# The first convolution's opening tiles moved into the end of the preceding group, and the loaded images put into another buffer

## The chip, the cores and the metric

The kernel runs on one core of a Trainium2 chip. The metric is the device time of one execution in microseconds (us). A core has five engines that run their own instruction streams side by side and wait for each other through semaphores: TensorE (PE in the rows; its weight loads are PEld), VectorE (DVE), ScalarE (ACT), GpSimd (POOL) and SyncE (SP, which here issues DMAs only). Data stands in an on-chip memory of 128 partitions (tensors `sb_...`) and in an accumulation memory that TensorE writes (`ps...`).

## The reference

The input is `x`, 16 images of 32 channels of 56 x 56 pixels. Cut to what matters here:

```
xn = group_norm(x)                       # 32 groups: each channel by itself
t2 = conv(xn, w2)                        # 1x3, 32 -> 32 channels
t3 = einsum(shifted xn, xn) / 56         # 7 Gram matrices of 32 x 32 per image
t7 = depthwise 1x5 of t2;  t8 = depthwise 5x5, dilation 2, of xn
t10 = einsum(p9w * p6w * t3, t2 shifted in rows) / sqrt(32 * 7)
x = x + t8 - (t10 - t7)
t = tokens of x                          # 3136 tokens of 32 per image
t = t + attention(layer_norm(t))         # one head
t = t + mixture_of_experts(layer_norm(t))
```

The changed part is the convolution stage ahead of the attention. Nothing of what it computes changes.

## The kernel before

Three stages follow each other: `prepare` (convolutions, Gram matrices, tokens, queries and keys), `attend` and `finish`. `prepare` takes the 16 images in four groups of four, so that 4 images x 32 channels fill 128 partitions. `step(g, new, old, more)` is written once per engine; step g does the convolutions of group g and beside them the tokens, keys and queries of the old group m = g - 1. A fifth step does the tokens of the last group.

For group g the order is as follows.

1. SP loads the four images into `XI` (`load`, L280). VectorE takes their mean and variance (`sample`, `statistics`) and writes the normalised images into the padded `Xp` (`normalise`, L786, semaphore `xp_ready`).
2. SP copies `Xp` into `XS` (tensor `sb_stacks`) in 16 strips for the first half of the rows and 16 for the second (`fill_stacks(g, 0)` and `fill_stacks(g, 1)`, L303, semaphores `xs_in[0]` and `xs_in[1]`). The first half may be written only when four of the old group's output tiles are done (`conv5_full`), the second only when all seven are.
3. An image has seven tiles of 448 pixels. TensorE's `conv3(g, i)` (L376) makes tile i of `t2` in the accumulation buffer `psA`, ScalarE's `to_t2` (L535) copies it into `T2`, and SP copies `T2` into a second set of strips `T2S` (`fill_stacks2`, L310, semaphores `t2s_in`).
4. `turn_stack` (L389) transposes strips on TensorE into `psT`, ScalarE's `turned` (L547) copies them to `TT`, and `correlate` (L397) multiplies them into the Gram matrices in `psG` (`gram_done`).
5. VectorE meanwhile works on `X1`, the output: `X1 = XI + tap` (L905), four more full-image taps (`taps5`), four taps of `T2` (`taps_row`, ends with `taps_done`), and between them the layer norms of the old group's tokens.
6. `conv5(g, i)` (L416) makes the seven output tiles in `psA`, and VectorE adds each to `X1` (`add`, L876, semaphore `x1_ready`).
7. `turn_output(g)` (L435) transposes all of `X1` into tokens: 25 transposes through two halves of `psT`, which ScalarE copies out (L676, L677). VectorE's next L905 overwrites `X1` and so waits until the last of these transposes is done (`t_full`).

Keys and queries of the old group are made by `turn_keys` and `queries` (L448, L460, L461), spread over the step; `queries` of the fourth image stand between `conv5` and `turn_output`. Below, the stretch from the end of `conv5(g, 6)` to the start of L905 of group g + 1 is called a changeover. There are three: from group 0 to 1, 1 to 2 and 2 to 3.

Before the change `XI` lies in the front of `T2`. So VectorE clears the padding of `T2` again in every group after L905 (L910 to L913, `t2_zero`), and the next images may be loaded only after `taps_done` and after `T2S` is filled. A program prints the functions here.

Of the kernel before, what the change touches and what calls it, by code (L numbers as in the profile page):

```python
# [15 lines left out]
N, C, H, W = 16, 32, 56, 56  # L16
P = 128
G = P // C
NG = N // G
T = H * W  # L20
TILE = 448
NT = T // TILE
# [126 lines left out]
def prepare(nc, x, wts, scr):  # L149
# [4 lines left out]
    with ExitStack() as ctx:  # L154
# [38 lines left out]

        XI = T2[:, 0:T]

# [82 lines left out]
        def _(sp):  # L278
# [48 lines left out]
            def step(g, new, old, more):  # L327
# [19 lines left out]
                if more:  # L347
                    sp.wait_ge(taps_done, g + 1)
                    for h in range(2):
                        sp.wait_ge(t2s_in[h], (g + 1) * STRIPS)  # L350
                    load(g + 1)
# [15 lines left out]
        def _(pe):  # L367
            def conv3(g, i):

                if i in (0, 3):  # L370
                    pe.wait_ge(xs_in[i // 3], (g + 1) * STRIPS)
                if i >= 2:
                    pe.wait_ge(t2_ready, g * NT + i - 1)
# [8 lines left out]
            def turn_stack(g, n, h):  # L382
                for k in HALVES[h]:
                    u = turned_set(n, h, k)
                    if u >= 2:
                        pe.wait_ge(t_free, g * TSETS + u - 1)
                    for q in range(G):
                        a = (XTOP + 2 * (G * k + q)) * XW
                        last = nc.tensor.transpose(psT[0:GR, u % 2, q * P:(q + 1) * P], XS[:, n, a:a + GR], ident[:])  # L389
                    last.then_inc(t_full, 1)  # L390
# [72 lines left out]
            def step(g, new, old, more):  # L463
# [12 lines left out]
                if not new:  # L476
# [5 lines left out]
                    return  # L482
                for i in range(3):
                    conv3(g, i)
                turn_stack(g, 0, 0)
# [34 lines left out]
                conv5(g, NT - 1, range(0, 4))  # L520
                conv5(g, NT - 1, range(4, 7), keys_of(3))
                run(queries_of(3))
                turn_output(g)

# [7 lines left out]
        def _(act):  # L532
            def to_t2(g, i):
                act.wait_ge(conv3_full, g * NT + i + 1)
                nc.scalar.activation(yrows(T2[:], YTOP + TR * i, YLEFT),  # L535
# [3 lines left out]
            def turned(g, n, h, part=slice(None)):  # L539
                place = (h * G + n) % 2  # L540
                if h * G + n >= 2:
                    act.wait_ge(gram_done, g * 2 * G + h * G + n - 1)
                for k in HALVES[h][part]:
                    u = turned_set(n, h, k)
# [37 lines left out]
            def step(g, new, old, more):  # L582
# [32 lines left out]
                if old:  # L615
# [3 lines left out]
                                  TM.rearrange("p n k c -> p n (k c)")).then_inc(tok_out, 16)  # L619
                act.wait_ge(t2_zero, g + 1)  # L620
                for i in range(3):
                    to_t2(g, i)
                if old:
# [37 lines left out]
                if old:  # L661
# [4 lines left out]
                    high_parts(m, 3, first[3])  # L666
                    keys(m, 3, first[3])
                    query_high(m, 3, range(QSETS), first[3])
                    act.wait_ge(res_out, m * G * 16 + G * 16)
                act.wait_ge(conv5_full, g * NT + NT)  # L670
# [40 lines left out]
        def _(dve):  # L711
# [18 lines left out]
            nc.vector.memset(wqk0[:], 0.0).then_inc(w_zero, 1)  # L730
            nc.vector.memset(Xp[:], 0.0)
            nc.vector.memset(X1[:, T:NC * P], 0.0)
            nc.vector.memset(lhs10[:], 0.0).then_inc(w_zero, 1)
# [132 lines left out]
            def step(g, new, old, more):  # L866
# [34 lines left out]
                if new:  # L901
                    dve.wait_ge(xp_ready, g + 1)
                    if old:
# [3 lines left out]
                    dve.wait_ge(xi_used, g + 1)  # L907

                    inside, end = YTOP * YW + YLEFT, (YTOP + H - 1) * YW + YLEFT + W
                    nc.vector.memset(T2[:, 0:inside], 0.0)  # L910
                    nc.vector.memset(T2[:, inside + W:inside + W + (H - 1) * YW].rearrange(
                        "p (r w) -> p r w", w=YW)[:, :, 0:YW - W], 0.0)
                    nc.vector.memset(T2[:, end:YLEN], 0.0).then_inc(t2_zero, 1)  # L913
                if old:
# [990 lines left out]
```

## Time and profile before

| | |
|---|---|
| time, median of 3 runs | 2673.1 us (2671.83 to 2673.99) |
| the profiled execution's own time, and its span | 2677.21 us, 2675.4 us |
| PE busy, DVE busy, ACT busy over the span | 2394.8, 2311.7, 1592.7 us |
| start of L905 in groups 0, 1, 2, 3 | 24.11, 138.78, 250.20, 360.69 us |
| start of the fifth step's work on VectorE (the last group's tokens) | 470.06 us |

The starts of L905 show a period: one group takes 111.42 us (250.20 - 138.78) and 110.49 us (360.69 - 250.20). The first group takes 114.67 us and does no old tokens.

### The profile page before, as it was taken

How to read it: one execution, taken by the hardware profiler on the slowest of the kernel's cores; microseconds unless marked ns; L12 is line 12 of the kernel's file. 1: busy time of each engine (PE TensorE's matmuls, PEld its weight loads, DVE VectorE, ACT ScalarE, POOL GpSimd, SP SyncE). 2: the span in 40 equal slices, each digit the busy share in tenths (PEclk: the TensorE clock that was granted, in tenths of full speed). 3: DMA queues.
4: the chain of work that ended last, by engine and by line, in shares of the span. 5: the costliest groups of instructions: out<-in, count | busy, mean ns of one | idle time of the engine just before them, and what ended most of it. 6: DMA issues, size and time to landing. Idle time of an engine off the chain costs nothing. (4 is left out here: it accounts for less than half of the span.)

```text
span 2675.4 us, 46972 instructions
## 1 busy us (share of the span) xinstructions
PE 2394.8 (90%) x18454; PEld 968.7 (36%) x18454; DVE 2311.7 (86%) x4151; ACT 1592.7 (60%) x2090; POOL 408.8 (15%) x456
## 2 busy tenths in 40 slices
PE   3878888269999999999999999999999998888886
PEld 1343343112222222222222222222222223878775
DVE  5486876699999999999999999999999993899997
ACT  1153443337777777777777777777777777243333
POOL 0021111300000001000000000000000000565666
PEclk9999999569999999999999999999999999676777
DMA  7697793420202212112022022020120001233230
GB/s 170 166 268 200 209 269 120 150 60 1 61 1 61 61 68 61 39 24 61 1 61 61 1 61 58 4 61 26 37 61 1 25 25 47 76 110 103 82 108 25
DMA packets 68110, 206.29 MB, mean 77 GB/s; under 512 B 20630, under 2 KB 33554, under 8 KB 61234
## 3 DMA queue, kind: packets, MB, share of 16 engines
q1 hardware_dynamic: 64034, 185.27, 25.3%
q0 software_dynamic: 3040, 15.57, 1.6%
q8 instruction: 145, 2.38, 0.4%
q10 hardware_dynamic: 816, 2.46, 0.3%
q14 instruction: 75, 0.61, 0.1%
HBM read 80.14 MB, written 61.31 MB: 53 GB/s over the span
## 5 line engine op out<-in xcount | busy, mean ns | idle before, releaser
L1395 DVE TENSOR_REDUCE at_XM<-at_psX 128x1 f32<-128x448 f32 x2688 | 1545.9, 620 | 89.2 <-PE at_psX L1220 68.4
L1301 ACT ACTIVATE at_PR<-at_psS 128x896 f32<-128x896 f32 x1344 | 1163.6, 915 | 454.1 <-PE at_psS L1196 452.1
L1238 PE MATMUL at_psV<-at_PR,at_V 128*32 128x448 f32 x5376 | 644.4, 551 | 0.1
L1196 PE MATMUL at_psS<-at_US,at_KS 128*128 128x448 f16 x2688 | 635.8, 356 | 1.2 <-ACT at_PR L1301 0.7
L1220 PE MATMUL at_psX<-at_KS,at_US 64*128 64x448 f16 x1344 | 489.7, 364 | 65.1 <-DVE at_XM L1395 43.0
L1220 PE MATMUL at_psX<-at_KS,at_UH 64*128 64x448 f16 x1344 | 489.7, 364 | 0.0
L1220 PEld LDWEIGHTS at_psX<-at_KS,at_US 64*128 64x128 f16 x1344 | 124.5, 93 | 719.8 <-DVE at_XM L1395 660.1
L1196 PEld LDWEIGHTS at_psS<-at_US,at_KS 128*128 128x128 f16 x2688 | 201.3, 98 | 271.6 <-ACT at_PR L1301 114.6
L1358 POOL CAST at_mrow<-at_mt 7x128 f16<-7x128 f32 x64 | 18.0, 281 | 1609.9 <-DVE at_mt L1414 1256.7
L1713 POOL TENSOR_TENSOR fi_WE<-fi_WE 128x256 f32<-128x256 f32 (+1 forms) x224 | 215.0, 986 | 99.7 <-DVE fi_WE L1767 99.5
L416 PE MATMUL psA<-sb_stacks,sb_lhs 128*32 128x448 f32 x1568 | 162.2, 560 | 8.8 <-DVE sb_X L876 8.8
L1238 PEld LDWEIGHTS at_psV<-at_PR,at_V 128*32 128x32 f32 x5376 | 105.7, 108 | 133.9 <-issue 125.1
L1767 DVE TENSOR_TENSOR fi_WE<-fi_psE,fi_WT 128x512 f32<-128x512 f32 (+1 forms) x208 | 128.3, 660 | 20.0 <-PE fi_psE L1599 18.1
L1568 PEld LDWEIGHTS fi_psO<-fi_wv,fi_SUMS 128*128 128x128 f32 x750 | 142.9, 293 | 3.4 <-issue 1.7
L1568 PE MATMUL fi_psO<-fi_wv,fi_SUMS 128*128 128x33 f32 x750 | 141.7, 361 | 1.3 <-DVE fi_T L1782 1.3
L1599 PE MATMUL fi_psE<-fi_wz,fi_ZS 128*128 128x256 f16 x400 | 97.2, 351 | 39.1 <-DVE fi_WE L1767 39.1
L1220 PEld LDWEIGHTS at_psX<-at_KS,at_UH 64*128 64x128 f16 x1344 | 124.5, 93 | 0.0
L705 POOL TENSOR_TENSOR sb_TK<-sb_TK,sb_XH 128x800 f32<-128x800 f32 x13 | 43.6, 3351 | 360.3 <-DVE sb_XH L818 360.3
L389 PE MATMUL psT<-sb_ident,sb_stacks 128*124 128x128 f32 x448 | 67.7, 295 | 26.9 <-ACT sb_TT L547 26.9
L416 PEld LDWEIGHTS psA<-sb_stacks,sb_lhs 128*32 128x32 f32 x1568 | 52.9, 111 | 100.8 <-issue 87.4
L1702 ACT ACTIVATE fi_ZS<-fi_psK 128x1024 f16<-128x1024 f16 x64 | 50.1, 837 | 58.5 <-PE fi_psK L1578 58.5
L376 PE MATMUL psA<-sb_stacks,sb_lhs 128*32 128x448 f32 x448 | 48.5, 564 | 37.7 <-DMA sb_stacks<-sb_Xp 32.3
(219 smaller groups left out, 1989.4 us busy)
## 6 DMA issues: line engine op xcount, KB each, us to landing
sums<-at_O SPq DMA_DIRECT2D x16, 1568.0 KB, 6.3
fi_SUMS<-sums SPq DMA_DIRECT2D x16, 1568.0 KB, 6.7
sb_stacks<-sb_T SPq DMA_DIRECT2D x64, 270.5 KB, 7.2
sb_stacks<-sb_Xp SPq DMA_DIRECT2D x64, 248.8 KB, 7.4
sb_stacks<-sb_Xp SPq DMA_DIRECT2D x64, 248.0 KB, 6.0
sb_stacks<-sb_T SPq DMA_DIRECT2D x64, 172.5 KB, 8.1
at_KS<-key_stacks SPq DMA_DIRECT2D x32, 208.0 KB, 6.9
fi_RES<-residual SPq DMA_DIRECT2D x16, 400.0 KB, 7.2
```

The costliest lines, as they stand in the source:

```text
L389: last = nc.tensor.transpose(psT[0:GR, u % 2, q * P:(q + 1) * P], XS[:, n, a:a + GR], ident[:])
L416: last = nc.tensor.matmul(o, w, v, start=(j == 0), stop=(j == 6))
L1196: last = nc.tensor.matmul(psS[:, at % 2, k, 0:TILE], KS[:, b, (2 * c + k) * P:(2 * c + k + 1) * P], US[:, b, t * TILE:(t + 1) * TILE], sta ...
L1220: last = nc.tensor.matmul(o, u[:, c * P:(c + 1) * P], k[:, t * TILE:(t + 1) * TILE], start=True, stop=True)
L1238: last = nc.tensor.matmul(psV[C * q:C * q + C, 0:TILE], V[:, b, G * k + q, :], PR[:, (n * 2 * STEPS + 2 * q4 + q // 2) % PRS, q % 2, :], s ...
L1301: nc.scalar.activation(PR[:, f % PRS], psS[:, at % 2, :, 0:TILE], ACT.Exp).then_inc(p_ready, 1)
L1395: nc.vector.tensor_reduce(o, psX[:, (at + j) % 3, 0:TILE], AX.X, ALU.max).then_inc(x_done, 1)
L1568: last = nc.tensor.matmul(psO[:, h, q * (C + 1):(q + 1) * (C + 1)], SUMS[:, b, k * P:(k + 1) * P], wv[:], start=True, stop=True)
L1599: last = nc.tensor.matmul(psE[:, u % 2, j * EC:(j + 1) * EC], ZS[:, b, a:a + P], wz16[:, 0:EC], start=True, stop=True)
L1702: nc.scalar.activation(ZS[:, b, a:a + w], psK[:, s % 2, 0:w], ACT.Copy).then_inc(zs_ready, 1)
L1713: return nc.gpsimd.tensor_tensor(WE[:, s, 0:h, 0:w], WE[:, s, 0:h, 0:w], WE[:, s, h:2 * h, 0:w], ALU.add)
L1767: nc.vector.tensor_tensor(WE[:, u // 2, :, q:q + j].rearrange("p e k c -> p k e c"), psE[:, u % 2, 0:j * EC].rearrange("p (k e c) -> p k e ...
```

## The change

`XI` moves from `T2` into the front of `TT`, the buffer of the turned strips. `T2` is cleared once at the start and no more after that. The load of the next images waits for `gram_done` (all strips of the group read) in place of `taps_done` and `T2S`. ScalarE's first two sets of `turned` wait until L905 has read `XI` (`xi_used`), and `to_t2` of tile 0 waits for `taps_done` and `T2S` of the group before. `conv3(g + 1, 0)`, `(g + 1, 1)` and `(g + 1, 2)` with their copies are issued at the end of step g, ahead of `turn_output(g)`, and no longer at the start of step g + 1.

```diff
-        XI = T2[:, 0:T]
+        XI = TT[:].rearrange("p a q s -> p (a q s)")[:, 0:T]
...
                 if more:
-                    sp.wait_ge(taps_done, g + 1)
-                    for h in range(2):
-                        sp.wait_ge(t2s_in[h], (g + 1) * STRIPS)
+                    sp.wait_ge(gram_done, (g + 1) * 2 * G)
                     load(g + 1)
...
                 if i in (0, 3):
                     pe.wait_ge(xs_in[i // 3], (g + 1) * STRIPS)
+                if i < 2 and g > 0:
+                    pe.wait_ge(x1_ready, g * NT - 1 + i)
...
                     if u >= 2:
                         pe.wait_ge(t_free, g * TSETS + u - 1)
+                    elif g > 0:
+                        pe.wait_ge(t_free, g * TSETS)
...
-                for i in range(3):
-                    conv3(g, i)
+                if not old:
+                    for i in range(3):
+                        conv3(g, i)
                 turn_stack(g, 0, 0)
...
                 conv5(g, NT - 1, range(4, 7), keys_of(3))
+                if more:
+                    conv3(g + 1, 0)
                 run(queries_of(3))
+                if more:
+                    conv3(g + 1, 1)
+                    conv3(g + 1, 2)
                 turn_output(g)
...
             def to_t2(g, i):
+                if i == 0:
+                    act.wait_ge(t2_zero, 1)
+                    if g > 0:
+                        act.wait_ge(taps_done, g)
+                        for h in range(2):
+                            act.wait_ge(t2s_in[h], g * STRIPS)
...
                 if h * G + n >= 2:
                     act.wait_ge(gram_done, g * 2 * G + h * G + n - 1)
+                else:
+                    act.wait_ge(xi_used, g + 1)
...
-                act.wait_ge(t2_zero, g + 1)
-                for i in range(3):
-                    to_t2(g, i)
+                if not old:
+                    for i in range(3):
+                        to_t2(g, i)
...
                     keys(m, 3, first[3])
+                if more:
+                    to_t2(g + 1, 0)
+                if old:
                     query_high(m, 3, range(QSETS), first[3])
+                if more:
+                    to_t2(g + 1, 1)
+                    to_t2(g + 1, 2)
...
             nc.vector.memset(Xp[:], 0.0)
+            nc.vector.memset(T2[:], 0.0).then_inc(t2_zero, 1)
...
-                    nc.vector.memset(T2[:, 0:inside], 0.0)
-                    nc.vector.memset(T2[:, inside + W:inside + W + (H - 1) * YW].rearrange(
-                        "p (r w) -> p r w", w=YW)[:, :, 0:YW - W], 0.0)
-                    nc.vector.memset(T2[:, end:YLEN], 0.0).then_inc(t2_zero, 1)
```

TensorE at the second changeover, before: the last output tile (L416), the fourth image's queries (L460, L461), the output's transposes (L435), then the next group's first convolution (L376) and strips (L389). A semaphore waited for stands in brackets.

```order
L416 MATMUL psA<-sb_stacks,sb_lhs 32x448 x4
L460 MATMUL psQ<-sb_KS,sb_mhi 128x416 [waits u_ready,ks_ready]
L461 MATMUL psQ<-sb_KS,sb_mlo 128x416
...
L435 MATMUL psT<-sb_ident,sb_X 128x128 [waits t_free,x1_ready]
L435 MATMUL psT<-sb_ident,sb_X 128x128 x3
...
L376 MATMUL psA<-sb_stacks,sb_lhs 32x448 [waits xs_in0]
L376 MATMUL psA<-sb_stacks,sb_lhs 32x448 x15
L376 MATMUL psA<-sb_stacks,sb_lhs 32x448 [waits t2_ready]
L376 MATMUL psA<-sb_stacks,sb_lhs 32x448 x7
L389 MATMUL psT<-sb_ident,sb_stacks 124x128 x8
```

The same place now (line numbers of the changed kernel: 418, 462, 463, 437 and 391 are the old 416, 460, 461, 435 and 389).

```order
L418 MATMUL psA<-sb_stacks,sb_lhs 32x448 x4
L376 MATMUL psA<-sb_stacks,sb_lhs 32x448 [waits x1_ready,xs_in0]
L376 MATMUL psA<-sb_stacks,sb_lhs 32x448 x7
L462 MATMUL psQ<-sb_KS,sb_mhi 128x416 [waits u_ready,ks_ready]
L463 MATMUL psQ<-sb_KS,sb_mlo 128x416
...
L376 MATMUL psA<-sb_stacks,sb_lhs 32x448 [waits x1_ready]
L376 MATMUL psA<-sb_stacks,sb_lhs 32x448 x7
L376 MATMUL psA<-sb_stacks,sb_lhs 32x448 [waits t2_ready]
L376 MATMUL psA<-sb_stacks,sb_lhs 32x448 x7
L437 MATMUL psT<-sb_ident,sb_X 128x128 [waits t_free,x1_ready]
...
L391 MATMUL psT<-sb_ident,sb_stacks 124x128 [waits t_free]
```

The wait for `xs_in0` moved from behind the output's transposes to a place ahead of the queries and of these transposes; all three tiles stand ahead of the transposes.

VectorE at the same changeover, before and now: the old group's last queries (L833, now L857), the first tap (L905, now L929), the first reduction of the new tokens (L804, now L828).

```order
L833 TENSOR_TENSOR sb_US<-psQ,sb_US 64x416 [waits u_hi] x4
L905 SCALAR_TENSOR_TENSOR sb_X<-sb_Xp,sb_w8e,sb_T 128x3136 [waits t_full,xp_ready,val_out]
L910 MEMSET sb_T 128x182 [waits xi_used]
L911 MEMSET sb_T 128x55x4
L913 MEMSET sb_T 128x190
L804 TENSOR_REDUCE sb_lsum<-sb_TK 128x25 [waits t_free]
```

```order
L900 TENSOR_TENSOR sb_X<-psA,sb_X 128x448 [waits conv5_full]
L857 TENSOR_TENSOR sb_US<-psQ,sb_US 64x416 [waits u_hi] x4
L929 SCALAR_TENSOR_TENSOR sb_X<-sb_Xp,sb_w8e,sb_TT 128x3136 [waits t_full,xp_ready,val_out]
L828 TENSOR_REDUCE sb_lsum<-sb_TK 128x25 [waits t_free,xi_used]
L829 TENSOR_SCALAR sb_lsum<-sb_lsum 128x25 [waits order]
```

Three clears left the stream; the first tap still waits for the last transpose (`t_full`).

## Rows read from the trace of the kernel before

**Rows 1.** Busy time by stretch: from:to, length, each engine's, granted clock, DMA share.
```profile
250.20:304.00 53.80, 41.30 (x486) 25.07 (x478) 49.43 (x42) 28.47 (x54) 12.84 (x7) 0.94 1.00 262
321.00:353.40 32.40, 31.88 (x319) 11.47 (x316) 16.79 (x36) 7.50 (x12) 3.56 (x4) 1.00 0.64 170
```

**Rows 2.** Timeline of VectorE: start, length, instruction, in brackets the idle time before it.
```profile
138.78 3.48 DVE L905 SCALAR_TENSOR_TENSOR sb_X<-sb_Xp,sb_w8e,sb_T 128x3136 f32<-128x3136 f32 x1 [4.78 <-PE psT L435]
...
250.20 3.48 DVE L905 SCALAR_TENSOR_TENSOR sb_X<-sb_Xp,sb_w8e,sb_T 128x3136 f32<-128x3136 f32 x1 [5.53 <-PE psT L435]
...
254.36 0.93 DVE L804 TENSOR_REDUCE sb_lsum<-sb_TK 128x25 f32<-128x800 f32 x1
...
360.69 3.49 DVE L905 SCALAR_TENSOR_TENSOR sb_X<-sb_Xp,sb_w8e,sb_T 128x3136 f32<-128x3136 f32 x1 [3.89 <-PE psT L435]
```

**Rows 3.** Timeline of TensorE at the three changeovers, the same columns.
```profile
132.35 0.98 PE L416 MATMUL psA<-sb_stacks,sb_lhs 128*32 128x448 f32 x8
134.06 1.09 PE L435 MATMUL psT<-sb_ident,sb_X 128*128 128x128 f32 x8 [0.73 <-DVE sb_X L876]
...
241.15 0.35 PE L460 MATMUL psQ<-sb_KS,sb_mhi 128*128 128x416 f16 x1
...
243.33 1.04 PE L435 MATMUL psT<-sb_ident,sb_X 128*128 128x128 f32 x8
...
249.98 3.26 PE L376 MATMUL psA<-sb_stacks,sb_lhs 128*32 128x448 f32 x32
...
256.74 0.43 PE L389 MATMUL psT<-sb_ident,sb_stacks 128*124 128x128 f32 x2
...
353.26 0.35 PE L460 MATMUL psQ<-sb_KS,sb_mhi 128*128 128x416 f16 x1
```

**Rows 4.** The last of 16 first-half strips, each changeover: its issue on SP's timeline.
```profile
129.45 0.72 SPq L303 DMA_DIRECT2D sb_stacks<-sb_Xp  x1
...
235.79 0.67 SPq L303 DMA_DIRECT2D sb_stacks<-sb_Xp  x1
...
348.30 0.73 SPq L303 DMA_DIRECT2D sb_stacks<-sb_Xp  x1
```

**Rows 5.** DMA issues of those three moments, in that order: the last number, us to landing.
```profile
sb_stacks<-sb_Xp SPq DMA_DIRECT2D x1, 248.0 KB, 9.2
...
sb_stacks<-sb_Xp SPq DMA_DIRECT2D x1, 248.0 KB, 10.4
...
sb_stacks<-sb_Xp SPq DMA_DIRECT2D x1, 248.0 KB, 9.3
```

**Rows 6.** DMA issues: the first strip, at 117.51 us, when no others were under way.
```profile
sb_stacks<-sb_Xp SPq DMA_DIRECT2D x1, 248.0 KB, 3.0
```

**Rows 7.** Group 0: timelines of SP, VectorE and TensorE, and last T2S strip's landing.
```profile
81.36 0.58 SPq L310 DMA_DIRECT2D sb_stacks<-sb_T  x1
...
sb_stacks<-sb_T SPq DMA_DIRECT2D x1, 270.5 KB, 12.9
...
82.97 0.95 PE L397 MATMUL psG<-sb_TT 124*32 124x128 f32 x28
...
94.36 0.38 SPq L280 DMA_DIRECT2D sb_T<-x  x1
...
101.29 2.21 DVE L773 BATCH_NORM_STATS2 sb_stats<-sb_T 128x6 f32<-128x448 f32 x4 [11.82 <-DMA sb_T<-x]
...
104.20 16.23 PE L416 MATMUL psA<-sb_stacks,sb_lhs 128*32 128x448 f32 x144 [7.57 <-DVE sb_X L876]
```

**Rows 8.** Busy time by stretch, behind TensorE's 7.57 us of idle time; granted clock third last.
```profile
104.20:109.10 4.90, 4.90 (x28) 1.42 (x32) 4.68 (x12) 0.20 (x1) 0.00 (x0) 0.50 0.02 3
109.10:118.00 8.90, 8.90 (x98) 3.31 (x94) 1.50 (x3) 0.00 (x0) 0.00 (x0) 1.00 0.00 0
```

**Rows 9.** Timeline of VectorE: the start of the program.
```profile
1.86 3.38 DVE L731 MEMSET sb_Xp<- 128x3980 f32 x1 [0.78 <-issue]
...
9.76 0.44 DVE L737 COPY sb_adder<-sb_eye 128x32 f32<-128x32 f32 x4 [4.18 <-DMA sb_wqk<-wqk]
```

**Rows 10.** Timeline of VectorE: a wait for query sets in group 2.
```profile
280.54 0.59 DVE L833 TENSOR_TENSOR sb_US<-psQ,sb_US 64x416 f16<-64x416 f32 x1 [1.53 <-ACT sb_US L579]
```

More of the change, by code:

```diff
@@ L667, in step @@
                     keys(m, 3, first[3])
+                if more:
+                    to_t2(g + 1, 0)
+                if old:
                     query_high(m, 3, range(QSETS), first[3])
+                if more:
+                    to_t2(g + 1, 1)
+                    to_t2(g + 1, 2)
+                if old:
                     act.wait_ge(res_out, m * G * 16 + G * 16)
@@ L907, in step @@
                     dve.wait_ge(xi_used, g + 1)
-                    inside, end = YTOP * YW + YLEFT, (YTOP + H - 1) * YW + YLEFT + W
-                    nc.vector.memset(T2[:, 0:inside], 0.0)
-                    nc.vector.memset(T2[:, inside + W:inside + W + (H - 1) * YW].rearrange(
-                        "p (r w) -> p r w", w=YW)[:, :, 0:YW - W], 0.0)
-                    nc.vector.memset(T2[:, end:YLEN], 0.0).then_inc(t2_zero, 1)
                 if old:
```

## The prediction

> **What bounds the kernel now.** I read three views in this order. The sums by stretch come first, since a share over the whole span mixes three stages and the change touches one. Within a group of the first stage they show two regimes [rows 1]. From L905 to the end of the taps (250.20 to 304.00) VectorE is busy 49.43 of 53.80 us, so it sets the pace there and TensorE (41.30) has room. From 321.00 to 353.40 TensorE is busy 31.88 of 32.40 us with `conv5`, and VectorE has room. Between one group's `conv5` and the next group's L905 lies the changeover, and there I read VectorE's timeline: it sits idle 4.78, 5.53 and 3.89 us ahead of L905, each time until the last transpose of `turn_output` [rows 2]. So every microsecond by which `turn_output` ends later makes L905 later, and VectorE has no room behind it to catch up. The third view is the DMA issues, for the question when the strips that `conv3` reads are there.
>
> Only three things can therefore move the end: when `turn_output` ends at the three changeovers, what VectorE does in its regime, and the wait for the next images in group 0, where both engines stand still (VectorE 11.82 us, TensorE 7.57 us) [rows 7].
>
> **The wait that moves ahead.** `conv3(g + 1, 0)` needs the first 16 strips of the next group. Before, it stood behind `turn_output` and found them landed. Now it stands directly behind `conv5`. The last of the 16 is issued at 129.45, 235.79 and 348.30 us [rows 4] and lands 9.2, 10.4 and 9.3 us later [rows 5]: at 138.65, 246.19 and 357.60. `conv5` ends at 133.33 (132.35 + 0.98), and at 241.15 and 353.26, where the queries follow it [rows 3]. TensorE would so stand idle for 5.3, 5.0 and 4.3 us. Nothing in the change issues these strips earlier: they still wait for four finished output tiles, and the sixteen take their time from the issue of the first. Behind the waiting instruction on TensorE stand the fourth image's queries and `turn_output`; for the queries wait ScalarE, VectorE and SP's store, and SP issues the second half of the strips behind that store.
>
> **What stands between the landing and L905.** One tile of `conv3` takes 1.63 us (two tiles, 32 matmuls, in 3.26). The queries take 2.18 us (241.15 to 243.33), and ScalarE's copy of tile 0 ahead of them fits into their first half microsecond. `turn_output` with nothing else in its way takes 4.72 us from its start at 134.06 to L905 at 138.78 [rows 2, 3]. So L905 comes 9.61 us after the landing at the first changeover (3 x 1.63 + 4.72; group 0 has no queries) and 11.79 us after it at the others (3 x 1.63 + 2.18 + 4.72). The three conv3 tiles stood on TensorE in VectorE's regime before, where they cost nothing; now all of them are on the path.
>
> - First changeover: 138.65 less the gain of 1.5 in group 0 (below) is 137.15, plus 9.61 is 146.76, against 138.78: **+8.0**.
> - Second: 246.19 + 11.79 = 257.98, against 250.20: **+7.8**.
> - Third: 357.60 + 11.79 = 369.39, against 360.69: **+8.7**.
>
> The changes add up because each is counted from its own group's times. Together +24.5 us.
>
> **The granted clock.** The trace shows one idle time of TensorE of this kind: after the 7.57 us in group 0 the granted clock is 0.50 for another 4.90 us of work (the lower of the two levels, 1.2 GHz), then 1.00 [rows 7, 8]. In these 4.90 us it ran 28 matmuls; at the rate of the next row (98 in 8.90) they take 2.5 us, so the idle time cost 2.4 us more behind itself. Here the waits are 5 us. Bounds are 0 and 2.4 us per changeover; by length, 2.4 x 5.0 / 7.57, I take 1.6, three times: **+4.8**.
>
> **The clears of T2.** VectorE loses three memsets per group. L905 of group 2 ends at 253.68 and L804 starts at 254.36 [rows 2], 0.68 us; some 0.1 us of it, the settling of L905's result, stays. In groups 1 to 3: 3 x 0.6 = **-1.8**. In group 0 VectorE waits for ScalarE afterwards, so nothing is gained there. The one clear at the start, of 3728 columns, costs about 3.2 us by that of 3980 columns in 3.38, and lies in the 4.18 us in which VectorE waits for the weights [rows 9]. Without that cover it would cost its 3.2.
>
> **The load of the next images.** In groups 1 and 2 nobody waits for it, so its earlier issue gains nothing there. In group 0 it is issued at 94.36, and its data is used at 101.29, 6.9 us later [rows 7]. Now it can be issued when the last Gram matmul is done, at about 83.9 (82.97 + 0.95), ten microseconds earlier. But on the same queue stand the strips of T2S, the last issued at 81.36 and landing at 94.3 (+ 12.9). Behind them the load needs its own transfer. Of its 6.9 us at most 3.0 are not transfer, since a lone strip lands in that time [rows 6]; so it lands between 98.2 and 101.2, a gain of 0 to 3.1, and I take the middle: **1.5**, already in the first changeover. VectorE's samples and first `add`, and `conv5(0, 2)` behind them, follow at the same distance. The Trainium skill, "DMA: Bandwidth & Descriptors", section "Queues, rings and completion order", says that transfers of one issuing engine are consumed in ring order but may complete out of order. By that the load might land ahead of the strips; this is one of the rivals.
>
> **Edits at no cost.** The waits of `turned` for L905 (`xi_used`): ScalarE reaches them behind `squares`, which needs VectorE's work after L905 anyway. The wait of `to_t2` for `taps_done` and `T2S` is long met at a changeover. The second half of the strips is issued later by some 6 to 7 us, since it follows the query store, but its reader `conv3(g, 3)` moves by 7 to 8 us too; if that cover were gone, each microsecond of lateness would be one on TensorE's path to the queries.
>
> **Sum.** 24.5 + 4.8 - 1.8 = +27.5 us. The profiled execution's own time is 2677.2 us, of which the span is 2675.4; it would become 2704.7. It lies 4.1 us above the median of the runs, and I put the same difference on the median: 2673.1 + 27.5 = **2700.6 us**, 1.0% slower. The likeliest case's own range is 2693 to 2706: 3 x 1.6 less without the clock, 3 x 0.8 more with it whole, and the load's 1.5 either way.
>
> **The rivals.**
> - *The strips are there in time.* Then `conv3` starts where `conv5` ends. L905 comes at 133.33 - 1.5 + 9.61 = 141.44, at 241.15 + 11.79 = 252.94 and at 353.26 + 11.79 = 365.05: +2.7, +2.7 and +4.4. With the clears, and no clock loss, +8.0: 2681 us. For it: the three tiles are then cover for nothing but themselves, and a lighter queue might speed the strips. Against: their first issue hangs on the same output tile as before, and 5 us would have to vanish.
> - *The head start is given back (not slower).* TensorE no longer does 6.76 us of `conv3` and waits between `turn_output` and the strips' transposes (249.98 to 256.74) [rows 3]. If TensorE paced the group from there, and the wait of 1.5 us for query sets went too [rows 10], 8.3 us would come back per group: 27.5 - 24.9 = +2.6, 2675.7 us, no change that can be measured. It decides from 7.4 us per group, (27.5 - 5.3) / 3. Against it: VectorE idles only 4.37 of 53.80 us there [rows 1], so no more than that can come back before the clears.
> - *The load overtakes the strips.* Then group 0 gains the whole 7.57 us of TensorE's idle time in place of 1.5: 2694.5 us. Against it: the landing of the last strip 12.9 us after its issue, four times that of a lone one, says that the engines were full until then.
> - *The clock falls in the group's first half too.* TensorE then idles from `turn_output` until ScalarE is done with `squares`, and its strips' transposes may run at the lower level and hold up the keys. Three times up to 2.4 us at each of two places: 14.4 in place of 4.8, 2710 us. For it: [rows 8]; against it: that work stands where TensorE has room.
>
> **Chances.** The forecast 0.76, strips in time 0.08, head start 0.05, the load overtaking 0.04, clock 0.07. The range of 2684 to 2709 leaves out the first two rivals and the far end of the last, under 2 in 10. A measurement of this kernel can tell about 0.2%, 5.3 us, from no change. Slower: 0.92, that is all but the head start and part of the strips in time (+8.0 is 0.3%). Same: 0.05. Faster: 0.03, if the head start and a load that overtakes came together.
>
> **What would show it.** In the profile after: an idle time of TensorE ahead of the first `conv3` matmul of each changeover of some 4 to 5 us, ended by the strips' DMA, with a granted clock of 0.50 behind it; VectorE's idle time ahead of its first tap at 12 to 14 us in place of 4 to 5.5; no clears behind that tap; the images' load of group 1 issued at about 84 us and TensorE's idle time of 7.57 us shortened by 0 to 3 us; the stretch from the first tap to the end of the taps the same to a microsecond. The prediction is wrong if the strips land by the end of `conv5`, or if that stretch is shorter by several microseconds.

## The result and the profile after

The changed kernel takes 2707.13 us (median of 4 runs, 2701.29 to 2709.75); the kernel before took 2673.49 us beside it (4 runs, 2671.83 to 2673.99). The ratio is 1.0128, with a 95% interval of 1.0115 to 1.014: slower by 1.3%, 33.6 us between the medians. Measured again on another chip it is 2705.83 us (4 runs, 2705.27 to 2709.29) against 2674.33, ratio 1.0114 [1.0099, 1.0129], 31.5 us. The profiled execution of the changed kernel is the fastest of its runs, 2701.29 us with a span of 2699.2.

The head of the page and its clock row:

```profile
span 2699.2 us, 46975 instructions
PE 2405.1 (89%) x18454; PEld 974.1 (36%) x18454; DVE 2313.3 (86%) x4140; ACT 1593.1 (59%) x2090; POOL 408.1 (15%) x456
...
PEclk9989989759999999999999999999999999677777
```

The span grew by 23.8 us, TensorE's busy time by some 10, VectorE's by 1.6 (2394.8 and 2311.7 before). TensorE has the same matmuls (x18454 in both), and they take longer; VectorE lost twelve short clears and got one long one. The rest of the span's growth is idle time. Where it lies, VectorE's timeline shows. It answers to [rows 2]; L900 is the last `add` of `conv5`, L929 the first tap.

```profile
130.34 0.62 DVE L900 TENSOR_TENSOR sb_X<-psA,sb_X 128x448 f32<-128x448 f32 x1 [4.66 <-PE psA L418]
147.42 3.48 DVE L929 SCALAR_TENSOR_TENSOR sb_X<-sb_Xp,sb_w8e,sb_TT 128x3136 f32<-128x3136 f32 x1 [16.45 <-PE psT L437]
150.94 0.99 DVE L828 TENSOR_REDUCE sb_lsum<-sb_TK 128x25 f32<-128x800 f32 x1
...
197.74 3.48 DVE L863 SCALAR_TENSOR_TENSOR sb_X<-sb_T,sb_w7e,sb_X 128x3136 f32<-128x3136 f32 x1
...
249.18 0.62 DVE L900 TENSOR_TENSOR sb_X<-psA,sb_X 128x448 f32<-128x448 f32 x1 [4.47 <-PE psA L418]
257.70 1.61 DVE L857 TENSOR_TENSOR sb_US<-psQ,sb_US 64x416 f16<-64x416 f32 x3 [7.90 <-ACT sb_US L595]
266.79 3.48 DVE L929 SCALAR_TENSOR_TENSOR sb_X<-sb_Xp,sb_w8e,sb_TT 128x3136 f32<-128x3136 f32 x1 [6.73 <-PE psT L437]
...
367.02 0.62 DVE L900 TENSOR_TENSOR sb_X<-psA,sb_X 128x448 f32<-128x448 f32 x1 [4.48 <-PE psA L418]
375.64 2.36 DVE L857 TENSOR_TENSOR sb_US<-psQ,sb_US 64x416 f16<-64x416 f32 x4 [8.00 <-ACT sb_US L595]
384.71 3.48 DVE L929 SCALAR_TENSOR_TENSOR sb_X<-sb_Xp,sb_w8e,sb_TT 128x3136 f32<-128x3136 f32 x1 [6.71 <-PE psT L437]
...
487.00 0.62 DVE L900 TENSOR_TENSOR sb_X<-psA,sb_X 128x448 f32<-128x448 f32 x1 [4.47 <-PE psA L418]
```

From here on a changeover is measured on VectorE: from the end of the last `add` to the start of the next first tap. After: 147.42 - 130.96 = 16.5, 266.79 - 249.80 = 17.0, 384.71 - 367.64 = 17.1, together 50.5 us. The first is one idle time; the other two are cut in two by the old queries (7.90 + 6.73 us of idle time at the second, where 5.53 stood ahead of the first tap before, and 8.00 + 6.71 at the third). The last `add` of the stage ends at 487.62.

TensorE at the same places answers to [rows 3]: L418 is `conv5`, L376 `conv3`, L437 `turn_output`, L462 the queries, L391 the strips' transposes.

```profile
135.80 6.97 PE L376 MATMUL psA<-sb_stacks,sb_lhs 128*32 128x448 f32 x48 [5.54 <-DMA sb_stacks<-sb_Xp]
142.69 1.09 PE L437 MATMUL psT<-sb_ident,sb_X 128*128 128x128 f32 x8
...
154.61 2.91 PE L391 MATMUL psT<-sb_ident,sb_stacks 128*124 128x128 f32 x12 [5.75 <-ACT sb_TT L563]
...
253.42 3.13 PE L376 MATMUL psA<-sb_stacks,sb_lhs 128*32 128x448 f32 x16 [4.31 <-DMA sb_stacks<-sb_Xp]
256.49 0.35 PE L462 MATMUL psQ<-sb_KS,sb_mhi 128*128 128x416 f16 x1
...
258.81 3.28 PE L376 MATMUL psA<-sb_stacks,sb_lhs 128*32 128x448 f32 x32
262.02 1.09 PE L437 MATMUL psT<-sb_ident,sb_X 128*128 128x128 f32 x8
...
370.98 3.21 PE L376 MATMUL psA<-sb_stacks,sb_lhs 128*32 128x448 f32 x16 [4.02 <-DMA sb_stacks<-sb_Xp]
```

At each changeover TensorE stands still ahead of the first `conv3` matmul, for 5.54, 4.31 and 4.02 us, and the strips' DMA ends it. The x of these rows counts records: a `conv3` tile has 8 matmuls and 16 records, so that the 32 and 28 matmuls of the prediction are records too. The matmuls behind the wait are slow: three tiles (48 records) take 6.97 us at the first changeover, one tile (16) takes 3.13 and 3.21 at the others, where two tiles (32) take 3.28 a little later. The sums by stretch (columns as in [rows 1]) give the clock of these places; they answer to [rows 8].

```profile
133.50:140.30 6.80, 4.50 (x28) 1.21 (x32) 0.00 (x0) 0.55 (x1) 0.00 (x0) 0.50 1.04 235
140.30:150.50 10.20, 7.33 (x61) 4.12 (x53) 3.08 (x1) 4.97 (x16) 0.00 (x0) 1.00 1.01 230
150.50:164.20 13.70, 8.52 (x59) 6.46 (x62) 13.06 (x14) 6.33 (x12) 4.03 (x1) 0.50 0.92 270
...
253.40:256.60 3.20, 3.18 (x17) 0.71 (x18) 0.00 (x0) 0.00 (x0) 0.00 (x0) 0.54 0.17 69
...
371.00:374.20 3.20, 3.20 (x17) 0.65 (x18) 0.00 (x0) 0.00 (x0) 0.00 (x0) 0.50 0.08 30
```

Behind each wait the granted clock is at 0.50 to 0.54, its lower level (1.2 GHz), and one tile takes 3.2 us at it in place of 1.63. It falls once more behind 150.50: TensorE idles for 5.75 us between `turn_output` and the strips' transposes.

The load of the next images, by its DMA issue (the line is the DMA view's) and by VectorE's first use of it; it answers to [rows 7].

```profile
sb_TT<-x SPq DMA_DIRECT2D x1, 1568.0 KB, 14.2
```

```profile
98.12 2.21 DVE L797 BATCH_NORM_STATS2 sb_stats<-sb_TT 128x6 f32<-128x448 f32 x4 [8.77 <-DMA sb_TT<-x]
```

It is issued at 83.87, about ten microseconds earlier, and is used at 98.12 in place of 101.29: the use came 3.2 us earlier.

### The profile page after: what moved, and what is told of

It is laid out like the page before. It is cut to its first block and busy times, and to the rows that moved or that the text cites. A ratio compares the mean times of both kernels' runs of the same rounds, so it can differ in the third digit from the quotient of the medians.

```text
span 2699.2 us, 46975 instructions
## 1 busy us (share of the span) xinstructions
PE 2405.1 (89%) x18454; PEld 974.1 (36%) x18454; DVE 2313.3 (86%) x4140; ACT 1593.1 (59%) x2090; POOL 408.1 (15%) x456
## 5 line engine op out<-in xcount | busy, mean ns | idle before, releaser
L1319 ACT ACTIVATE at_PR<-at_psS 128x896 f32<-128x896 f32 x1344 | 1163.4, 915 | 455.9 <-PE at_psS L1214 454.0
L418 PE MATMUL psA<-sb_stacks,sb_lhs 128*32 128x448 f32 x1568 | 158.1, 549 | 5.8 <-DVE sb_X L900 5.8
L391 PE MATMUL psT<-sb_ident,sb_stacks 128*124 128x128 f32 x448 | 75.1, 319 | 41.0 <-ACT sb_TT L563 39.5
L376 PE MATMUL psA<-sb_stacks,sb_lhs 128*32 128x448 f32 x448 | 53.6, 616 | 45.7 <-DMA sb_stacks<-sb_Xp 45.7
L418 PEld LDWEIGHTS psA<-sb_stacks,sb_lhs 128*32 128x32 f32 x1568 | 49.1, 110 | 98.6 <-issue 88.3
```

The lines of the kernel that those rows point to most:

```text
L418: last = nc.tensor.matmul(o, w, v, start=(j == 0), stop=(j == 6))
L1319: nc.scalar.activation(PR[:, f % PRS], psS[:, at % 2, :, 0:TILE], ACT.Exp).then_inc(p_ready, 1)
```

## The experiments

The new order does two things at a changeover: it puts TensorE behind strips that are not there, and it puts three convolution tiles ahead of `turn_output`. Three more parts were thought to be small: the clock, the load and the clears. The theory is the prediction's sum; its rivals are that the buffer's move costs something of its own, or that the waits and tiles hide each other. The kernel before was run beside each kernel on its chip.

### One tile ahead of the turn, not three

Only `conv3(g + 1, 0)` stays ahead; the other two stand at the start of the next step, as before.

```diff
-                if not old:
-                    for i in range(3):
-                        conv3(g, i)
+                for i in range(1 if old else 0, 3):
+                    conv3(g, i)
...
-                if more:
-                    conv3(g + 1, 1)
-                    conv3(g + 1, 2)
                 turn_output(g)
...
```

> The changed kernel with only the first conv3 tile ahead of the turned tokens, the other two back at the start of a step. My theory (wait for the strips, then every tile on the path): the wait stays, 2 x 1.63 us leave the path at three changeovers, 2707.1 - 9.8 = 2697.3 us. Rival (the number of tiles is all the loss, the wait is hidden): a third of the loss is left, some 2685. Rival (the wait is all the loss): 2707, no change.

Measured: 2694.83 us (4 runs, 2689.75 to 2696.57) against 2673.82, ratio 1.0072 [1.0057, 1.0088]. TensorE at the first changeover:

```profile
127.76 3.59 PE L418 MATMUL psA<-sb_stacks,sb_lhs 128*32 128x448 f32 x36
136.94 0.98 PE L376 MATMUL psA<-sb_stacks,sb_lhs 128*32 128x448 f32 x4 [5.59 <-DMA sb_stacks<-sb_Xp]
```

The wait is whole with one tile (5.59 us), and the two tiles are worth some 11 us (2705.83 - 2694.83; 12.3 from the first result): about twice 1.63 for each of three changeovers, 9.8. In the profiles the changeovers are 10.1 us shorter (table at the end of this part). They hide in nothing.

### The strips in time

In groups 1 to 3 only the first 8 of the 16 strips of the first half are copied, so the convolution of these groups works on old data in the other 8; all matmuls remain.

```diff
-                for n, s in STRIP_ORDER:
+                for n, s in STRIP_ORDER[0:len(STRIP_ORDER) if g == 0 or h == 1 else len(STRIP_ORDER) // 2]:
...
-                    pe.wait_ge(xs_in[i // 3], (g + 1) * STRIPS)
+                    pe.wait_ge(xs_in[i // 3], (g + 1) * STRIPS if i == 3 else STRIPS + g * STRIPS // 2)
```

> The changed kernel, with only 8 of the 16 first-half strips copied in groups 1 to 3 (the others keep the strips of the group before, so the results of these groups are not the reference's). The strips then land before conv5 ends. My theory: the waits of 5.5 + 4.3 + 4.0 us and the lower clock behind them (about 2 us each) go, the tiles ahead of the turned tokens stay: 2707.1 - 13.9 - 6 = 2687 us. Rival (the tiles are all the loss): 2707. Rival (the wait is all the loss): 2673.

Measured: 2685.22 us (9 runs, 2679.6 to 2689.96) against 2674.33, ratio 1.0036 [1.0025, 1.0047]. TensorE's timeline, first changeover:

```profile
127.52 2.10 PE L418 MATMUL psA<-sb_stacks,sb_lhs 128*32 128x448 f32 x20
129.43 4.76 PE L376 MATMUL psA<-sb_stacks,sb_lhs 128*32 128x448 f32 x48
134.12 1.09 PE L437 MATMUL psT<-sb_ident,sb_X 128*128 128x128 f32 x8
```

With the strips there, `conv3` follows `conv5` without a gap, and the three tiles take 4.76 us in place of 6.97: the slow tiles came with the wait. Against the changed kernel on the same chip this is 2705.83 - 2685.22 = 20.6 us less; what is left, +10.9, is put down to the three tiles (its changeovers are 11.6 us longer than those of before). The wait and the lower clock behind it go together here, so this kernel doesn't part the two; and it moves half the bytes of the first half, so what a lighter queue is worth by itself isn't parted from them either.

### Both at once

One tile ahead and half the strips, so the same old data in groups 1 to 3. The diff is that of the two above.

> The changed kernel with one conv3 tile ahead of the turned tokens (as e3) and 8 of the 16 first-half strips in groups 1 to 3 (as e4, so these groups' results are not the reference's). My theory (the wait and each tile are separate terms): 2685.2 less 2 x 1.63 us at three changeovers, 2675.4 us, and TensorE has no wait for strips. Rival (without the wait the tiles lie in time that TensorE has at the changeover): 2685, as e4.

Measured: 2674.48 us (12 runs, 2669.49 to 2676.73) against 2674.33 (17 runs), ratio 0.9997 [0.9988, 1.0007]. TensorE, first changeover:

```profile
127.58 3.64 PE L418 MATMUL psA<-sb_stacks,sb_lhs 128*32 128x448 f32 x36
130.98 1.75 PE L376 MATMUL psA<-sb_stacks,sb_lhs 128*32 128x448 f32 x16
132.66 1.09 PE L437 MATMUL psT<-sb_ident,sb_X 128*128 128x128 f32 x8
```

The four kernels make a square (they ran on three chips, on which the kernel before took 2673.82 to 2674.33):

| | strips late | half the strips | difference |
|---|---|---|---|
| three tiles ahead | 2705.83 | 2685.22 | 20.6 |
| one tile ahead | 2694.83 | 2674.48 | 20.4 |
| difference | 11.0 | 10.7 | |

Waits and tiles add up and neither hides the other. By the intervals each difference is known to some 4 to 6 us; the changeovers of the profiles say the same more closely, 10.1 us for two tiles with the strips late and 9.7 with half of them. The first tile with its strips there costs nothing that can be seen in the time; the three changeovers are 1.9 us longer than before (20.9 against 19.0), where 4.9 would be the tile's full length three times. At the first changeover part of it lies in the 0.73 us in which TensorE waited for the last `add` anyway [rows 3].

### The queries ahead of the tiles

```diff
                 conv5(g, NT - 1, range(4, 7), keys_of(3))
-                if more:
-                    conv3(g + 1, 0)
                 run(queries_of(3))
                 if more:
-                    conv3(g + 1, 1)
-                    conv3(g + 1, 2)
+                    for i in range(3):
+                        conv3(g + 1, i)
...
```

> The changed kernel with the fourth image's queries ahead of all three conv3 tiles. My theory: the queries' 2.2 us then run inside the wait for the strips at the second and third changeover, 2707.1 - 4.4 = 2702.7 us, and idle time ahead of conv3 there falls from 4.3 and 4.0 to about 2 us. Rival (the wait for the strips is hidden, work is the price): no change, 2707.

Measured: 2700.52 us (4 runs, 2697.03 to 2701.41) against 2673.82, ratio 1.0095 [1.0081, 1.0109]. TensorE at the second and the third changeover:

```profile
251.47 0.34 PE L463 MATMUL psQ<-sb_KS,sb_mlo 128*128 128x416 f16 x1
254.32 6.46 PE L376 MATMUL psA<-sb_stacks,sb_lhs 128*32 128x448 f32 x48 [2.51 <-DMA sb_stacks<-sb_Xp]
260.72 1.09 PE L437 MATMUL psT<-sb_ident,sb_X 128*128 128x128 f32 x8
...
372.60 4.79 PE L376 MATMUL psA<-sb_stacks,sb_lhs 128*32 128x448 f32 x48 [1.48 <-DMA sb_stacks<-sb_Xp]
```

The queries fill part of the wait: it falls from 4.31 to 2.51 us and from 4.02 to 1.48. So much of the cost at these two changeovers came from queries that were ready and stood behind a tile that wasn't. The three tiles are slow behind 2.51 us of idle time (6.46 us), but not behind 1.48 (4.79).

### The clock kept up

Sixteen matmuls on data that is there, into a bank whose content nobody reads then, between `conv5` and the first `conv3` tile.

```diff
+        KEEP = 4
...
                 if more:
+                    for r in range(KEEP):
+                        for n in range(G):
+                            nc.tensor.matmul(psG[C * n:C * n + C, 0:TILE], lhs2[:, 0, :], XI[:, r * TILE:(r + 1) * TILE],
+                                             start=True, stop=True)
                     conv3(g + 1, 0)
```

> The changed kernel with 16 matmuls without use (3.6 us) at each changeover, between conv5 and the first conv3 tile, so that TensorE works while the strips land. My theory (the clock falls in the wait, and the tiles behind it run slower, 6.97 us for three in place of 4.89): 2 us less per changeover, 2701 us, and runs that lie as close together as those of before. Rival (the clock's fall is off the path): no change, 2707. Rival (the matmuls outlast the wait): slower than 2707.

Measured: 2701.2 us (4 runs, 2698.4 to 2702.91) against 2674.33, ratio 1.009 [1.0073, 1.0107]. TensorE's timeline; L529 are the added matmuls (32 records for 16), L377 and L438 the old L376 and L437:

```profile
129.73 3.18 PE L529 MATMUL psG<-sb_TT,sb_lhs 128*32 128x448 f32 x32
135.20 4.79 PE L377 MATMUL psA<-sb_stacks,sb_lhs 128*32 128x448 f32 x48 [2.28 <-DMA sb_stacks<-sb_Xp]
139.91 1.09 PE L438 MATMUL psT<-sb_ident,sb_X 128*128 128x128 f32 x8
...
251.95 1.73 PE L377 MATMUL psA<-sb_stacks,sb_lhs 128*32 128x448 f32 x16 [1.07 <-DMA sb_stacks<-sb_Xp]
...
371.41 1.73 PE L377 MATMUL psA<-sb_stacks,sb_lhs 128*32 128x448 f32 x16 [1.16 <-DMA sb_stacks<-sb_Xp]
```

The strips come no sooner (3.18 + 2.28 = 5.46 us from `conv5` to the first tile), but the tiles run at full speed: 4.79 us for three, 1.73 for one. So at the changeovers the clock's share is shown apart from the wait. The kernel is 4.6 us faster than the changed one on the same chip, and the ranges of their four runs don't meet there (the slowest 2702.91, the fastest 2705.27); the changed kernel's first result, on another chip, reaches down to 2701.29.

That this gain in time is the gain of the changeovers is not shown. In the profiles they are 6.0 us shorter, but the first stage ends only 0.9 us earlier, because the part of a group from the end of the taps to the last `add` got longer. Here it is for group 1, the changed kernel first, then this one (columns as in [rows 1]):

```profile
201.22:249.80 48.58, 45.77 (x454) 15.06 (x443) 31.29 (x67) 10.68 (x18) 6.55 (x7) 1.00 0.63 182
```

```profile
198.15:248.57 50.42, 48.28 (x474) 15.94 (x466) 31.28 (x66) 10.88 (x18) 6.54 (x7) 0.97 0.60 178
```

Over groups 1 to 3 this part takes 151.0 us at a granted clock of 0.97 in each, in the two profiles of the changed kernel 146.3 and 147.0. What brought the clock down there is not shown.

### The buffer and the load alone

`conv3` and its copies go back to the start of the step; the buffer, the early load and the single clear stay.

```diff
-                if not old:
-                    for i in range(3):
-                        conv3(g, i)
+                for i in range(3):
+                    conv3(g, i)
...
-                if more:
-                    conv3(g + 1, 0)
                 run(queries_of(3))
-                if more:
-                    conv3(g + 1, 1)
-                    conv3(g + 1, 2)
                 turn_output(g)
...
```

> The changed kernel with the three conv3 tiles and their copies back at the start of a step; the images in TT, the early load and the single clear of T2 stay. My theory (the loss is the tiles and their wait for the strips ahead of the turned tokens): no loss is left, group 0 gains the 3.1 us that the load now lands earlier (98.1 in place of 101.3), the clears 1.8: 2668.6 us, against 2673.5 before. Rival (the loss lies in the buffer: ScalarE waiting until the first tap has read the images, or the load on the strips' queue): still above 2690. Rival (the gains are covered): 2673.

The second kernel is this one with the old conditions for the load put back:

```diff
+                    sp.wait_ge(taps_done, g + 1)
+                    for h in range(2):
+                        sp.wait_ge(t2s_in[h], (g + 1) * STRIPS)
```

> As e1, but the load of the next images waits for the taps and for T2S again, as before. My theory: only the clears' 1.8 us are left as a gain, 2671.7 us, so that the difference to e1 is the load's 3.1. Rival (the load's earlier landing is covered by the strips or by conv5): the same time as e1.

Measured: 2673.7 us (11 runs, 2667.67 to 2677.15), ratio 0.9995 [0.9986, 1.0004], and 2673.02 us (11 runs, 2667.77 to 2676.61), ratio 0.9993 [0.9984, 1.0002], both against 2673.82 (21 runs). The first interval holds 2670.1 to 2674.9, so the expected 2668.6 is refuted. The second, 2669.5 to 2674.4, holds the expected 2671.7, but the 3.1 us expected between the two kernels are not there (0.7, the other way). Neither kernel can be told from the kernel before, nor from each other. VectorE's rows of the first, with the early load:

```profile
99.12 2.21 DVE L783 BATCH_NORM_STATS2 sb_stats<-sb_TT 128x6 f32<-128x448 f32 x4 [9.26 <-DMA sb_TT<-x]
...
131.40 0.62 DVE L886 TENSOR_TENSOR sb_X<-psA,sb_X 128x448 f32<-128x448 f32 x1 [4.66 <-PE psA L418]
136.80 3.48 DVE L915 SCALAR_TENSOR_TENSOR sb_X<-sb_Xp,sb_w8e,sb_TT 128x3136 f32<-128x3136 f32 x1 [4.77 <-PE psT L437]
```

and of the second, with the late one:

```profile
100.05 1.68 DVE L786 BATCH_NORM_STATS2 sb_stats<-sb_TT 128x6 f32<-128x448 f32 x3 [10.50 <-DMA sb_TT<-x]
```

The early load is there at 99.12, the late one at 100.05, that of before at 101.29: a microsecond or two, and nothing of it can be seen in the time. The buffer's move costs nothing that can be measured either (by the first interval at most 1.1 us, net of what the load and the clears gain); the rival above 2690 is refuted.

### Both kernels again

> The changed kernel once more, for a second profile of it: its four runs lie 8.5 us apart, those of before 2.2. My theory (the idle times at the changeovers drop the granted clock, and how long it stays low differs from run to run): a slower profile than 2701 shows the same idle times ahead of conv3 (5.5, 4.3, 4.0 us) and the additional time in stretches with a granted clock of 0.50 behind them. Rival (the DMA's speed differs from run to run): the strips land later.

> The kernel before once more, for a second profile. The medians of the two kernels lie 33.6 us apart, their profiles 23.8. My theory (single executions lie some 3 us to either side by where the granted clock is low): this profile's first stage ends between 460 and 465 us as in the first (463.55), its changeovers are the same to half a microsecond, and what differs lies in stretches of a granted clock of 0.50. Rival (the change also makes the attention or the last stage longer): from the last add to the end of the span this profile takes clearly less than the 2211 to 2215 us of the changed kernel's two.

> A third profile of the kernel before, for the same question: my theory's spread of 2 to 3 us between the three spans, or the rival's common offset behind the first stage.

The changed kernel measured 2705.83 us (told above), its span 2703.1; the kernel before 2671.63 and 2673.08 us in single runs, spans 2669.8 and 2671.3. VectorE in the first of these two, where L876 is the last `add` and L905 the first tap of each changeover:

```profile
132.50 0.62 DVE L876 TENSOR_TENSOR sb_X<-psA,sb_X 128x448 f32<-128x448 f32 x1 [4.67 <-PE psA L416]
137.91 3.48 DVE L905 SCALAR_TENSOR_TENSOR sb_X<-sb_Xp,sb_w8e,sb_T 128x3136 f32<-128x3136 f32 x1 [4.78 <-PE psT L435]
...
238.71 0.62 DVE L876 TENSOR_TENSOR sb_X<-psA,sb_X 128x448 f32<-128x448 f32 x1 [4.47 <-PE psA L416]
...
246.54 3.48 DVE L905 SCALAR_TENSOR_TENSOR sb_X<-sb_Xp,sb_w8e,sb_T 128x3136 f32<-128x3136 f32 x1 [4.43 <-PE psT L435]
...
457.44 0.62 DVE L876 TENSOR_TENSOR sb_X<-psA,sb_X 128x448 f32<-128x448 f32 x1 [4.48 <-PE psA L416]
```

Its changeovers are 4.8, 7.2 and 6.4 us. By the same rows of every profile:

| profile | three changeovers, us | last `add` of the stage ends | from there to the span's end |
|---|---|---|---|
| before (the one of the prediction) | 19.7 | 463.6 | 2211.8 |
| before, again | 18.4 | 458.1 | 2211.8 |
| before, again | 18.9 | 459.3 | 2212.0 |
| changed | 50.5 | 487.6 | 2211.6 |
| changed, again | 51.0 | 488.6 | 2214.6 |
| clock kept up | 44.8 | 487.2 | 2213.6 |
| queries first | 43.7 | 485.8 | 2213.5 |
| one tile | 40.7 | 477.2 | 2215.0 |
| half the strips | 30.6 | 465.9 | 2211.6 |
| one tile, half the strips | 20.9 | 461.0 | 2213.5 |
| buffer alone | 18.5 | 458.5 | 2211.9 |
| buffer alone, late load | 19.2 | 455.9 | 2209.8 |

The means of the stage's end, 460.3 before (three profiles) and 488.1 after (two), lie 27.8 us apart.

The expectations here were mostly missed. The changed kernel's second profile is 3.9 us longer than its first, but the idle times ahead of `conv3` are 5.34, 4.98 and 4.16 us, the changeovers together only 0.5 us longer, and 3.0 of the 3.9 us lie behind the first stage; so the additional time isn't found behind the waits. Of the kernel before, the stage ends at 458.1 and 459.3 us and not between 460 and 465, the second changeover is 7.2 and not 8.3 us, and the three spans lie 5.6 us apart and not 2 to 3. Where they differ was expected rightly: in two groups the part from the end of the taps to the last `add` was slower in the first profile, at a lower clock. Group 2, in the first profile and in the second:

```profile
303.50:354.03 50.53, 48.28 (x467) 16.90 (x456) 31.28 (x67) 11.01 (x19) 6.56 (x7) 0.97 0.61 176
```

```profile
299.84:348.08 48.24, 46.07 (x443) 16.40 (x440) 31.26 (x66) 10.66 (x18) 6.54 (x7) 1.00 0.62 184
```

The rival (a longer last part in the changed kernel) has no sign of its own here: from the stage's end on, the kernel before takes 2211.8 and 2212.0 us, the changed one 2211.6 and 2214.6.

## Why the prediction was right, point by point

The direction and the mechanism were right, and the time is inside the range of 2684 to 2709, 6.5 us above the point forecast (5.2 by the second measurement). The narrower range of the likeliest case, 2693 to 2706, was missed by 1.1 us (the second measurement lies in it); by the terms given for it, it would have been 2694.3 to 2704.5.

- **The wait that moves ahead: right.** Forecast were 5.3, 5.0 and 4.3 us of idle time of TensorE, ended by the strips; measured 5.54, 4.31 and 4.02. That the strips' landing sets it is shown by the kernel with half of them, in which the idle time is gone, and by the one with added matmuls, in which the strips land no sooner.
- **What stands between the landing and L905: right.** Two of the three tiles are worth 11.0 and 10.7 us at either kind of strips, forecast 9.8. That all three are on the path holds with the strips late; with the strips there the first tile is partly hidden (1.9 of 4.9 us).
- **The granted clock: right.** Forecast +4.8 us, three times 1.6. In the profile the tiles behind the waits take 6.89 us (135.80 to 142.69) for three where 4.89 were reckoned, and about 3.07 (253.42 to 256.49) and 3.2 for one in place of 1.63: 2.0 + 1.4 + 1.6 = 5.0. Keeping the clock up made the tiles fast again and the changeovers 6.0 us shorter; of the time it gave back 4.6 us.
- **The changeovers' sum: right.** The terms of 8.0 + 7.8 + 8.7, without the load's 1.5 that is in the first, and with the clock, come to 30.8 us; the measured sums grew from 19.0 (mean of three profiles) to 50.8 (mean of two), 31.8. The sign given for it, 12 to 14 us of VectorE's idle time ahead of the first tap, was narrower than the prediction's own terms, by which it is 15.9 us at the first changeover (4.78 + 8.0 + 1.5 + 1.6); measured 16.45, 14.63 and 14.71.
- **The load: mis-sized, and unimportant.** The Trainium skill, "DMA: Bandwidth & Descriptors", section "Queues, rings and completion order", leaves it open whether a later transfer of a ring ends before an earlier one. Here the load, queued behind the strips of `T2S`, did not overtake them: the last strip landed at 94.5 us (81.47 + 13.0), the load at 98.1 (83.87 + 14.2). VectorE had its images 3.2 us earlier in the profile, the upper bound of 0 to 3.1 and not the middle. The buffer alone shows no gain in the time.
- **The clears of T2: not confirmed.** Forecast -1.8. The instructions are gone (L828 starts at 150.94, 0.04 us behind L929), but the stretch from the first tap to the end of the taps of group 1 takes 53.8 us (147.42 to 201.22) where it took 53.3. Over groups 1 to 3 it takes 159.85 us, before 159.86; with the buffer alone 158.52, and with the late load 159.29. So where the rest is as before 0.6 to 1.3 us may be gained, and in the changed kernel it is lost again. The one clear at the start takes 3.17 us and is covered, as forecast: the first tap starts at 24.16 us, before at 24.11.
- **The clock in the group's first half, a rival: there, but small.** The clock is 0.50 from 150.50 to 164.20, as the rival said, behind an idle time of 5.75 us. It held up the work little: the three stretches together are as long as before, so it can have cost about what the clears gave. The measured time lies nearer to this rival's 2710 than to the forecast; these rows, not the time, speak against it.
- **The head start given back, the load overtaking, the strips in time:** refuted by the changeovers' rows, by the load's, and by the idle time ended by the strips.

The first stage so came out at +27.8 us in the profiles, forecast +27.5. That the two agree so closely is in part luck. The changeovers grew by 31.8 us in place of 30.8, the first group ended 2.8 us earlier in place of 1.5, and the stretches from the first tap to the end of the taps gave 0.1 us in place of 1.8. The other 1.1 us is the slow first profile of the kernel before, which the prediction was made from; against its other two profiles the stage is 29.4 us longer.

The medians lie 31.5 and 33.6 us apart, and 3.7 to 5.8 us of this are not found in the first stage. Part of it is which executions were profiled: the changed kernel's two profiled runs lie 5.8 and 0.6 us under the medians of their runs. The time from the stage's end to the span's end, where no instruction was changed, averages 2213.7 us in the five profiles in which TensorE waits for strips and 2211.8 in the other seven, but among these seven alone it spans 2209.8 to 2213.5. Among single runs of one kernel the time goes with the granted clock of the whole run: with the changed kernel from 0.927 in the fastest (2701.29 us) to 0.923 in the slowest (2709.75), with the kernel before from 0.936 (2668.81) to 0.930 (2680.36). What sets the clock of a single run stays open, and with it the rest. The failed part of the forecast is the step from one profiled execution to the median: it carried the +27.5 over unchanged, where the medians lie 31.5 to 33.6 us apart.

## What to carry to other kernels

Before work is moved to an earlier place in an engine's order, read when the last transfer that it needs lands there, not only whether the engine has the time: an in-order engine that meets a transfer not yet landed keeps everything behind it, here 14 us of idle time and 5 us of lower clock. Work that lay in a stretch in which another engine sets the pace cost nothing there (that stretch is no shorter without it, 159.85 us against 159.86); ahead of the instruction that this other engine waits for it costs its full length (each of the two added tiles 5.4 us over the three changeovers). And time the parts by themselves: here the two large ones simply added up, and the two small gains could not be seen in the time at all.

## What the runs showed of the hardware

- Sixteen matmuls that compute nothing useful, run in a wait that was there anyway, kept the granted clock at its upper level behind the wait (tiles of 1.73 us in place of 3.13). The changeovers became 6.0 us shorter and the time 4.6 us; in the profiles most of the 6.0 was lost again where the clock was lower later in the groups.
- From the end of the taps to the last `add` of a group, where TensorE is busy 46 to 48 us, the kernel before took 48.1 to 48.2 us at a granted clock of 1.00 and 49.9 to 50.5 at 0.97 (groups 1 and 2, three profiles).
- The load landed 14.2 us after its issue when it stood behind the strips. In the buffer kernel with the late load the same 1568 KB landed 6.4 us after the issue, and VectorE had them only 0.9 us later than with the early one: most of an earlier issue went into standing in the queue.

The DMA view of that kernel has the row:

```profile
sb_TT<-x SPq DMA_DIRECT2D x1, 1568.0 KB, 6.4
```

- Single runs of one kernel lie up to 11.6 us apart (the kernel before, 2668.81 to 2680.36 in 17 runs on one chip). Profiles of the same kernel differ in the first stage's end by 5.5 us (458.1 to 463.6), more than the small terms of this sum.
